# Where a group's last tile is split and projected in a streamed attention

## The reference

```python
q, k = _rmsnorm(q, q_norm_w), _rmsnorm(k, k_norm_w)
qg = q.reshape(b, HKV, G, s, HD)
scores = jnp.einsum('bkgqd,bksd->bkgqs', qg, k) / math.sqrt(HD)
bias = jnp.where(rel > 0, NEG_INF, slopes[:, :, None, None] * rel)
attn = jax.nn.softmax(scores + bias[None], axis=-1)
out = jnp.einsum('bkgqs,bksd->bkgqd', attn, v)
return out.transpose(...).reshape(b, s, H * HD) @ Wo.T
```

## Time and profile before

| | us |
|---|---|
| median of 3 runs (lowest, highest) | 1589.75 (1589.71, 1590.87) |
| the profiled execution | 1590.18 |
| its span, first to last instruction | 1588.2 |
| TensorE busy with matmuls | 1500.3 (94%) |
| VectorE busy | 1111.3 (70%) |
| ScalarE busy | 795.4 (50%) |
| GpSimd busy | 440.1 (28%) |
| step 0 of the streamed stage starts at | 492.4 |
| step 9 starts / step 10 starts / step 11 starts at | 631.3 / 646.6 / 658.8 |

### The profile page before, as it was taken

One profiled execution on the slowest core, in us unless ns is written; L12 is line 12 of the kernel. 1 busy time (PEld: TensorE's weight loads), 2 busy tenths in 40 slices (PEclk: granted clock), 3 DMA queues, 4 the chain that ended last, 5 costly groups with the idle time before them and its releaser, 6 DMA issues.

```text
span 1588.2 us, 25452 instructions
## 1 busy us (share of the span) xinstructions
PE 1500.3 (94%) x8968; PEld 1169.6 (74%) x8968; DVE 1111.3 (70%) x2866; ACT 795.4 (50%) x2087; POOL 440.1 (28%) x435
## 2 busy tenths in 40 slices
PE   3998999998898999999999999999999999999998
PEld 2863444443686888888888888888888888888776
DVE  5658777772576786677677678678767767767873
ACT  3522555557334555555555555555455555555441
POOL 4102000010444141441332323134134133234333
PEclk9997999999999999999999999999999999999999
DMA  4364344301101000100100100010010010000000
GB/s 151 96 140 58 41 57 59 49 2 55 54 21 40 1 28 1 40 28 1 41 14 14 33 9 27 1 41 27 1 40 28 1 41 14 14 21 21 3 25 27
DMA packets 40205, 54.25 MB, mean 34 GB/s; under 512 B 5776, under 2 KB 21392, under 8 KB 40080
## 3 DMA queue, kind: packets, MB, share of 16 engines
q1 hardware_dynamic: 40080, 52.65, 14.0%
HBM read 44.04 MB, written 8.39 MB: 33 GB/s over the span
## 4 chain that ended last, share of the span: by engine, by line
PE 65%; DVE 4%; issue 2%; ACT 2%; POOL 2%; POOLq 0%; ACTq 0%; DVEq 0%
PE ps L50 19%; PE ps L52 18%; PE ps L51 18%; PE ps L1530 7%; PE ps L1505 2%; DVE ab_qt_l L1780 1%; POOL ab_o_l L1426 1%; PE ps L241 0%; PE ps L1507 0%; ACT ab_kt_h L1676 0%; ACT ab_o_raw L1697 0%; DVE ab_pt_l L1788 0%; POOL ab_o_h L1424 0%; ACT ab_squares L1667 0%; DVE prob L1771 0%
## 5 line engine op out<-in xcount | busy, mean ns | idle before, releaser
L1655 ACT ACTIVATE prob<-prob,ab_neg_max 128x128 f32<-128x128 f32 (+7 forms) x256 | 200.8, 785 | 238.4 <-DVE ab_neg_max L1771 237.0
L1788 DVE TENSOR_TENSOR ab_pt_l<-ps,ab_pt_h 128x512 fp32r<-128x512 f32 x288 | 198.0, 688 | 64.5 <-ACT ab_pt_h L1683 62.2
L1683 ACT CAST ab_pt_h<-ps 128x512 fp32r<-128x512 f32 x288 | 171.7, 596 | 124.4 <-PE ps L1530 123.8
L1771 DVE CUSTOM_DVE_ANT_0 prob<-ps,rel 128x512 f32<-128x512 f32 (+3 forms) x256 | 146.1, 571 | 99.4 <-PE ps L52 98.7
L1041 DVE TENSOR_REDUCE ra_part_max<-ps 128x1 f32<-128x512 f32 (+3 forms) x318 | 156.5, 552 | 47.1 <-PE ps L943 28.0
L50 PE MATMUL ps<-ab_w_h,ab_xt_h 128*128 128x512 f32 (+1 forms) x512 | 184.3, 360 | 2.4 <-DVE ab_v_l L1808 2.4
L1530 PE MATMUL ps<-ident,prob 128*128 128x128 f32 x1152 | 173.4, 273 | 1.4
L52 PE MATMUL ps<-ab_w_h,ab_xt_l 128*128 128x512 f32 (+1 forms) x512 | 173.6, 339 | 0.0
L51 PE MATMUL ps<-ab_w_l,ab_xt_h 128*128 128x512 f32 (+1 forms) x512 | 172.8, 337 | 0.0
L1796 DVE TENSOR_SCALAR prob<-prob,ab_recip 128x128 f32<-128x128 f32 (+7 forms) x256 | 164.1, 641 | 9.1
L1413 POOL TENSOR_TENSOR ab_rms<-ab_ms_eps,neg_half 128x5 f32<-128x5 f32 x64 | 76.3, 1192 | 303.5 <-DVE ab_ms_eps L1813 302.6
(11 more groups left out here) (232 smaller groups left out, 3479.4 us busy)
## 6 DMA issues: line engine op xcount, KB each, us to landing
f_raw<-in_wqkv SPq DMA_DIRECT2D x32, 384.0 KB, 3.7
f_raw<-in_wbo SPq DMA_DIRECT2D x32, 256.0 KB, 2.6
ra_first_rows<-parts SPq DMA_DIRECT2D x36, 128.0 KB, 6.9
parts<-pa_stage SPq DMA_DIRECT2D x12, 256.0 KB, 3.0
parts<-f_raw SPq DMA_DIRECT2D x12, 256.0 KB, 3.3
ra_q_st<-parts SPq DMA_DIRECT2D x24, 128.0 KB, 6.8
ra_k_st<-parts SPq DMA_DIRECT2D x24, 128.0 KB, 7.0
f_raw<-in_wf SPq DMA_DIRECT2D x8, 324.0 KB, 3.3
```

What stands on the lines that cost most here:

```text
L1655: act.activation(prob[:, t % 2, h, 0:w], prob[:, t % 2, h, 0:w], ACT.Exp, bias=neg_max[:, t % 2, h, pieces_per_head(t % NT) - 1:pieces_per ...
L1683: act.copy(pt_h[:, n % PT, :], ring_bank("p", u, j)).then_inc(pt_high, 1)
L1771: dve.tensor_tensor_reduce(out=prob[:, t % 2, h, k0:k1], in0=ps[:, n % 2, a:b], in1=const["rel"][:, SLIDE - i * P + k0:SLIDE - i * P + k1] ...
L1788: dve.tensor_tensor(pt_l[:, n % PT, :], ring_bank("p", u, j), pt_h[:, n % PT, :].bitcast(F32), ALU.subtract).then_inc(emptied, 1)
```

## The change

Six edits in `stream_block` and its plan:

1. `mixed_in`: for tile 0 of a group the only block is mixed four slots later, in slot 0 of step u + 2 (was slot 4 of step u + 1). `taken_in` follows by itself.
2. For the last tile of a group, but not of the last group (`at_once`: tiles 7, 15, ..., 55), ScalarE casts bank 7 straight to `o_h`, and VectorE, in slot 4 behind its shift, subtracts `o_h` from bank 7 for `o_l`. GpSimd leaves these tiles out, and the count of `o_out` skips them (`copies_before`).
3. `output_in`: these tiles are projected in slot 0 of step u + 3 (was slot 7 of step u + 2), after the mix of tile u + 1, and both before the slot's project. VectorE's residual addition moves with it.
4. Tile u + 1 may mix when `o_l` of tile u is done.
5. The four casts of the new output weights on ScalarE stand together in slot 1 of step 2 of the group (were two in slot 7 of step 1 and one each in slots 0 and 1 of step 2).
6. ScalarE's q copy and key copy signal `qk_high` each for itself, and VectorE waits for each apart.

```diff
 def mixed_in(t, s):
     u, j = (t - 1, s - 4) if s >= 4 else (t - 2, s + B_SLOTS - 4)
-    return (u, j) if 0 <= u < B_STEPS and j <= u % NT else None
+    if u % NT == 0:
+        j -= 4
+    return (u, j) if 0 <= u < B_STEPS and 0 <= j <= u % NT else None
+def at_once(u):
+    return u % NT == NT - 1 and u < B_STEPS - NT
+def output_in(t, s):
+    u = t - 3 if s == 0 else t - 2
+    return u if s in (0, 7) and 0 <= u < B_STEPS and at_once(u) == (s == 0) else None
+def copies_before(u):
+    return u - u // NT
...
@@ gpsimd, slot 4
-                    if s == 4 and 0 <= t - 2 < B_STEPS:
-                        pool.wait_ge(o_out, t - 1)
+                    if s == 4 and 0 <= t - 2 < B_STEPS and not at_once(t - 2):
+                        pool.wait_ge(o_out, copies_before(t - 2) + 1)
@@ tensor, mix
-                        pe.wait_ge(o_out, u)
+                        if at_once(u - 1):
+                            pe.wait_ge(o_low, u)
+                        else:
+                            pe.wait_ge(o_out, copies_before(u))
@@ tensor, step
+                    if s == 0:
+                        if mixed_in(t, s):
+                            mix(*mixed_in(t, s))
+                        if output_in(t, s) is not None:
+                            project_out(output_in(t, s))
                     if s < KC and EARLY <= t + 2 < B_STEPS:
                         project(t + 2, s)
@@ scalar
-                act.copy(qt_h[...], ring_bank("q", t)...)
+                act.copy(qt_h[...], ring_bank("q", t)...).then_inc(qk_high, 1)
...
+                        if at_once(u):
+                            act.wait_ge(out_done, u)
+                            act.copy(o_h[:, :], ps[:, 7, :]).then_inc(o_high, 1)
+                        else:
...
-                    if i == 1 and s == 7 and 1 <= g < KVB:
+                    if i == 2 and s == 1 and 1 <= g < KVB:
                         act.wait_ge(out_done, NT * g)
-                        split_high_of(2 * KC * g + KC)
-                        split_high_of(2 * KC * g + KC + 1)
-                    if i == 2 and s < 2 and 1 <= g < KVB:
-                        split_high_of(2 * KC * g + KC + 2 + s)
+                        for k in range(KC):
+                            split_high_of(2 * KC * g + KC + k)
@@ vector
-                dve.wait_ge(qk_high, t + 1)
+                dve.wait_ge(qk_high, 2 * t + 1)
                 dve.tensor_tensor(qt_l[...], ...)
+                dve.wait_ge(qk_high, 2 * t + 2)
                 dve.tensor_tensor(kt_l[...], ...)
...
+                    if s == 4 and taken_in(t, s) is not None and at_once(taken_in(t, s)):
+                        u = taken_in(t, s)
+                        dve.wait_ge(o_high, u + 1)
+                        dve.tensor_tensor(o_l[:, :], ps[:, 7, :], o_h[:, :].bitcast(F32), ALU.subtract).then_inc(o_low, 1)
```

More of the change, by code:

```diff
@@ L1151, in shared_jobs @@
                 add(t, "p", *turned_in(t, s))
-            if s == 7 and 0 <= t - 2 < B_STEPS:
-                add(t, "o", t - 2)
+            if output_in(t, s) is not None:
+                add(t, "o", output_in(t, s))
             half, q = half_of(t, s)
@@ L1585, in step @@
                         turn(*turned_in(t, s))
+                    if s == 0:
+                        if mixed_in(t, s):
+                            mix(*mixed_in(t, s))
+                        if output_in(t, s) is not None:
+                            project_out(output_in(t, s))
                     if s < KC and EARLY <= t + 2 < B_STEPS:
                         project(t + 2, s)
-                    if mixed_in(t, s):
+                    if s and mixed_in(t, s):
                         mix(*mixed_in(t, s))
-                    if s == 7 and 0 <= t - 2 < B_STEPS:
-                        project_out(t - 2)
+                    if s and output_in(t, s) is not None:
+                        project_out(output_in(t, s))
                     second(*half_of(t, s))
@@ L1674, in qk_high_of @@
                 act.wait_ge(qk_turned, t + 1)
-                act.copy(qt_h[:, t % 2, :, :], ring_bank("q", t).rearrange("p (h t) -> p h t", h=GB))
+                act.copy(qt_h[:, t % 2, :, :], ring_bank("q", t).rearrange("p (h t) -> p h t", h=GB)).then_inc(qk_high, 1)
                 act.copy(kt_h[:, key_columns(t)], ring_bank("k", t)[:, 0:P]).then_inc(qk_high, 1)
@@ L1694, in step @@
                         act.wait_ge(mixed, blocks_before(u + 1))
-                        if u:
-                            act.wait_ge(o_low, u)
-                        act.copy(o_raw[:, :], ps[:, 7, :]).then_inc(o_out, 1)
+                        if at_once(u):
+                            act.wait_ge(out_done, u)
+                            act.copy(o_h[:, :], ps[:, 7, :]).then_inc(o_high, 1)
+                        else:
+                            if u:
+                                act.wait_ge(o_low, u)
+                            act.copy(o_raw[:, :], ps[:, 7, :]).then_inc(o_out, 1)
                     if turned_in(t, s):
@@ L1871, in step @@
                     second(*half_of(t, s))
-                    if s == 7 and 0 <= t - 2 < B_STEPS:
-                        u = t - 2
+                    if output_in(t, s) is not None:
+                        u = output_in(t, s)
                         dve.wait_ge(out_done, u + 1)
```

## The result

The changed kernel takes 1579.25 us at the median of four runs (1577.89 to 1580.11), and the kernel before, run beside it, 1590.31 (1589.71 to 1591.32). The ratio is 0.9928 with a 95% interval of 0.9913 to 0.9943: 11.1 us faster. Forecast were 1578.5 us in a range of 1576.6 to 1582.2. The profiled execution of the changed kernel took 1580.11 us with a span of 1578.0. A later repetition gave 1578.8, beside 1591.37 for the kernel before: 12.6 us less.

The account below looks back on a forecast made before the run. TensorE was taken to bound the kernel, with 65% of the chain that ended last. Gains of 7.1 + 2.6 + 1.5 = 11.2 us take the profiled 1590.18 to 1579.0, the median to 1578.5; range 1576.6 to 1582.2.

Parts of the forecast that it names:

- three causes: The forecast gain's parts: seven group borders 7.1 us, the q copy's signal 2.6, the clock in step 2 1.5.
- seven borders: Between groups of the streamed stage, TensorE's loss falls from 1.55 to 0.54 us each: 7.1 us, bounds 6.0 to 7.8.
- q copy's own signal: VectorE starts 0.16 us earlier, which counts at sixteen TensorE waits in steps 2 and 3 of groups: 2.6 us.
- clock in step 2: Tile 0's mix fills TensorE's idle time, so the granted clock does not fall in step 2: 1.53 us.
- 0.06 us for the signal: At a border, the time from the end of VectorE's read-out of (9,2) to TensorE's start on score (10,0).
- second full restart: At a border's mix, charged because its weights can't be loaded ahead: 0.10 us, bounds 0 and 0.25.
- The covers: Work around the border that must not be late: tile 11's scaling 0.58 us early, GpSimd's chain with 0.39 slack.
- The walk: Prediction's step-by-step timing at a border; GpSimd's chain ends at 654.41, leaving 0.39 us slack after the signal.
- GpSimd's splits become the wait: Rival: tile 8's low part 0.6 us late, TensorE waits 0.31 at seven places: 2.2 us, 1580.7; chance 0.12.
- What I had costed at nothing: GpSimd's splits holding up VectorE's normalisation of (10,0) after a border, by one split at most; charged no time.
- the slower rival: VectorE stretches six operations in GpSimd's chain by 0.38 each; TensorE waits 2.0 a border, 14.1 us: 1592.6; chance 0.03.

Follow-up runs that it names:

- e6: Changed kernel with one more GpSimd copy of 128x512 ahead of tile 8's cast at each border: 1581.32 us, ratio 0.9938 to the kernel before.
- e4: Changed kernel, TensorE's order kept, but tile 7's output copied by ScalarE and split by GpSimd as before: 1583.22 us, ratio 0.9949 to the kernel before.
- e1: Kernel before with only the q copy's own signal added: 1588.05 us, ratio 0.9982 to the kernel before.
- e2: Changed kernel with q and key copy signalling together again, as before: 1581.78 us, ratio 0.994 to the kernel before.
- e7: Changed kernel with the turn of the probabilities between the project's halves in slot 3 of steps 2 and 3 of each group: 1579.66 us.
- e3: Changed kernel with tile 0's mix put back into step 1 in the first group only: 1580.45 us, ratio 0.994 to the kernel before.
- e8: e7 with a mix and the first score between the project's halves at seven borders: 1575.08 us; repeated 1575.98, beside the changed kernel's 1578.8.
- e5: Changed kernel with mixes, projection and weight copies at their old places, keeping the ScalarE and VectorE split and q signal: 1587.23 us, ratio 0.9966 to the kernel before.

## Why the prediction was right

It was right in its three causes and in the sum; one of the terms, the border, came out to a few hundredths by luck.

| part | forecast | measured in the trace |
|---|---|---|
| seven borders | 7 x 1.01 = 7.1 | 7 x 1.03 = 7.2 |
| q copy's own signal | 16 x 0.16 = 2.6 | 16 x 0.167 = 2.7 |
| clock in step 2 | 1.5 | 3.72 - 2.20 = 1.5 |
| together | 11.2 | 11.4; from step 0 to the end 1095.78 - 1084.46 = 11.3 |

**The border** was right through two errors that cancel, and that is luck. I allowed 0.06 us for the signal behind VectorE's read-out. The read-out ends at 640.96 and TensorE starts at 641.11, so it took 0.15, and the loss is 0.42 instead of 0.34. I charged a second full restart of 0.10 at the mix, and it costs 0.02: VectorE starts `ab_o_l` together with the read-out, at 640.88, and ends 0.69 later, at 641.57, as walked. I had the result and the mix meet within 0.01 us; with the score started 0.09 later by its signal, the mix comes at 641.71, 0.14 behind the result, and that is enough to spare it the restart. That the earlier result is what spares it fits the trace and was not tried by itself. Forecast 0.54 a border, measured 0.42 + 0.08 + 0.02 = 0.52.

**The covers** held. Two came out as walked: tile 11's v 0.54 before its use (forecast 0.58), `ms_eps` 0.17 (0.16). GpSimd's chain was forecast with 0.39 us of slack after the signal and has 0.32, and e6 gives 0.32 too. The walk took the chain of four splits and tile 8's two operations over from the kernel before, 7.01 us; it takes 653.61 - 646.51 = 7.10, mainly because of the slower cast. The rival "GpSimd's splits become the wait" falls for the change. What I had costed at nothing in it is there without a price: the normalisation at 650.84 takes 0.92 us for 384 columns beside GpSimd's work (0.48 at this place before), and TensorE does not wait for it. The Trainium skill, "SBUF — State Buffer", section "Who interferes with whom", says that the engine of the two that starts first holds the shared ports for its whole instruction and the other stands still; the trace agrees for VectorE as the loser, with `ms_eps` at 0.73 in e4 and 0.17 after the change. It agrees for GpSimd as the loser too: the normalisation that started at 650.84 is still running when the cast starts at 651.49, and the cast takes 0.74 instead of the 0.60 that it takes when it starts first. In e6 the added copy stands in that place and takes 0.74 to 0.77 us at the seven borders, and the cast behind it 0.61. That the ports are the reason is read from the rule and these rows; no run takes the normalisation away. So the slower rival, by which GpSimd would be the loser, did show, but with 0.14 us in one operation of six and not 0.38 in each, and the cover took it: `ab_o_l` takes 1.30 at 652.31, its median of before.

**The signal** was sized by the wait that disappears, 0.16 of 0.29, and not by the whole wait. e1 and e2 show the same 0.17, with and without the rest of the change, and the rest of the wait is there for e7 to take.

**The clock** was the term with the least behind it, one stretch of the trace in which shorter idle pieces left the clock at 1.00. e3 shows that it was right: with the mix back the fall is back, 1.54 us.

The forecast was 0.75 below the median, and the profiled execution 1.1 above the 1579.0 forecast for it. Ahead of step 0 its span holds 1578.0 - 1084.46 = 493.5 us against 1588.2 - 1095.78 = 492.4 before: the 1.1 lies there, in code that the change doesn't touch.

## What to carry to other kernels

Count a stall from start to start of the matmuls, with the restart behind it, and follow it to the engine that ends last: at a border that was 1.55 us where the idle figures say 1.0. When a wait is moved, price the next operation in line as carefully as the one removed (here VectorE's read-out of the score bank), and write down the slack of each cover in tenths of a us: the walk of the thinnest one was 0.07 off (0.39 forecast, 0.32 measured), because an operation taken over at its old length now had a neighbour that started before it. Moving an operation and making it faster gave 0.55 and 0.16 us a border apart and 1.03 together, so judge such edits as a pair.

## What the runs showed of the hardware that was not expected

The stage ahead of step 0 is the same in all kernels, yet its length varied from 491.5 to 495.9 us. It goes with the clock. In the window from 400 to 490 us the granted clock is 0.98 in the kernel before and in e6, which has the shortest stage, 0.96 in the changed kernel (second window above), and 0.94 in e4 and e7, which have two of the three longest. The third is the repetition of e8. Windows of e6, of e7, and two of the repetition of e8:

```profile
400.00:490.00 90.00, 80.69 (x463) 66.88 (x452) 58.16 (x163) 27.53 (x76) 44.55 (x60) 0.98 0.10 33
```

```profile
400.00:490.00 90.00, 82.69 (x461) 68.22 (x460) 56.52 (x155) 27.18 (x75) 41.91 (x55) 0.94 0.10 33
```

```profile
400.00:490.00 90.00, 81.89 (x463) 66.89 (x461) 57.84 (x162) 27.95 (x77) 42.32 (x57) 0.96 0.11 33
491.20:494.60 3.40, 3.40 (x16) 3.40 (x17) 0.29 (x1) 0.54 (x2) 1.18 (x1) 0.50 0.00 0
```

In the last one TensorE runs at 0.50 for 3.4 us just ahead of step 0. Added up over the stage, the clock records of the traces have TensorE at the lower level for 23.9 us in e3 and e6 (stages of 492.0 and 491.5 us), for 27.3 to 30.7 us in seven others (492.4 to 494.2), and for 34.1 us in e4, e7 and the repetition of e8 (495.4 to 495.9). In this stage TensorE stops often, and the falls do not lie at the same places in all executions, while the one in step 2 comes whenever the mix stands in step 1. So changes of one or two us can only be read here from the stage that they touch. What decides where it falls stays open.

The other surprise is small: the signal from VectorE's read-out to TensorE's score took 0.15 us, where ScalarE's copy reached the mix in 0.06 (copy ended at 641.63, mix at 641.69) and VectorE's subtraction in e5 reached it in 0.05 (ended at 642.92, mix at 642.97).
